# A gated cross-attention and channel-mix kernel: the inverse root of stage two in twelve links on VectorE, right behind the moments, from the second unit on

## The reference

```python
def _layernorm(x, axis=-1, eps=1e-05):
    m = jnp.mean(x, axis=axis, keepdims=True)
    v = jnp.var(x, axis=axis, keepdims=True)
    return (x - m) / jnp.sqrt(v + eps)
...
def _reference_tuple_inner(x, W_r, W_k, W_v, mu_r, mu_k):
    x_prev = jnp.concatenate([jnp.zeros((B, 1, C), x.dtype), x[:, :-1, :]], axis=1)
    xr = mu_r * x + (1.0 - mu_r) * x_prev
    xk = mu_k * x + (1.0 - mu_k) * x_prev
    r = jax.nn.sigmoid(jnp.einsum('btc,dc->btd', xr, W_r))
    k = jnp.einsum('btc,dc->btd', xk, W_k)
    k_act = jnp.square(jax.nn.relu(k))
    out = r * jnp.einsum('btc,dc->btd', k_act, W_v)
...
x = x + jnp.tanh(g_xattn[0]) * _L0_xattn_ref(_layernorm(x, axis=-1), ctx_1024, ctx_1024, mask_SxS2_bk1, ...)
x = x + jnp.tanh(g_ffn[0]) * _L0_ffn_ref(_layernorm(x, axis=-1), L0_ffn_W_r, L0_ffn_W_k, L0_ffn_W_v, L0_ffn_mu_r, L0_ffn_mu_k)
```

## Time and profile before

| what | value |
|---|---|
| median of 3 runs | 1153.17 us (1152.59 to 1156.04) |
| profiled execution, whole | 1153.75 us |
| its span, first to last instruction | 1151.9 us |
| mean granted clock of PE | 0.997 |
| PE busy | 1118.8 us, 97% of the span |
| DVE busy | 888.4 us, 77% |
| ACT busy | 686.3 us, 60% |
| POOL busy | 367.6 us, 32% |

### The profile page before, as it was taken

One profiled execution on the slowest core, in us unless ns is written; L12 is line 12 of the kernel. 1 busy time (PEld: TensorE's weight loads), 2 busy tenths in 40 slices (PEclk: granted clock), 3 DMA queues, 4 the chain that ended last, 5 costly groups with the idle time before them and its releaser, 6 DMA issues.

```text
span 1151.9 us, 21580 instructions
## 1 busy us (share of the span) xinstructions
PE 1118.8 (97%) x7216; PEld 895.2 (78%) x7216; DVE 888.4 (77%) x1964; ACT 686.3 (60%) x1527; POOL 367.6 (32%) x595
## 2 busy tenths in 40 slices
PE   5999999999999999999999999979999999999998
PEld 4677777777778778777877777757888888888886
DVE  7878877888788878887888788867677776776764
ACT  4767776777677767776777677753333323332232
POOL 0153153045045026116214302663442334323331
PEclk9999999999999999999999999989999999999999
DMA  8675575764775676567567557702311132111300
GB/s 284 199 199 146 166 212 153 193 193 132 199 203 131 192 207 171 139 196 214 149 168 211 141 144 229 222 12 74 99 55 56 55 95 71 55 55 62 103 20 37
DMA packets 95709, 162.48 MB, mean 141 GB/s; under 512 B 13296, under 2 KB 22640, under 8 KB 95472
## 3 DMA queue, kind: packets, MB, share of 16 engines
q1 hardware_dynamic: 84912, 143.37, 44.0%
q10 hardware_dynamic: 10688, 17.73, 5.4%
HBM read 109.91 MB, written 49.57 MB: 138 GB/s over the span
## 4 chain that ended last, share of the span: by engine, by line
PE 87%; DMA 3%; issue 2%; DVE 2%; POOL 1%; ACT 1%; SPq 0%; DVEq 0%; ACTq 0%; POOLq 0%
PE bank L550 26%; PE bank L624 18%; PE bank L586 14%; PE bank L615 10%; PE bank L636 9%; PE bank L594 8%; PE bank L749 1%; DMA w_raw<-wvvT 1%; ACT kact_hi L985 1%; PE bank L738 1%; DMA rden_dram<-ctx_sb 0%; DVE xh L1238 0%; POOL w2r_lo L1429 0%; DVE kact L1276 0%; DMA qk_dram<-q_hi 0%
## 5 line engine op out<-in xcount | busy, mean ns | idle before, releaser
L904 ACT ACTIVATE probs<-neg_s,negmax 128x512 f32<-128x512 f32 x512 | 368.1, 720 | 65.0 <-DVE negmax L1079 62.7
L1079 DVE CUSTOM_DVE_ANT_0 neg_s<-bank,mask_big 128x512 f32<-128x512 f32 x512 | 344.0, 679 | 9.7 <-DVE mask_big L1139 1.0
L624 PE MATMUL bank<-ident,probs 128*128 128x128 f32 x2048 | 307.6, 273 | 3.0 <-DVE pT L1085 2.9
L624 PEld LDWEIGHTS bank<-ident,probs 128*128 128x128 f32 x2048 | 248.1, 140 | 51.1 <-issue 6.1
L1085 DVE COPY pT<-bank 128x512 f32<-128x512 f32 x254 | 175.0, 689 | 110.2 <-PE bank L624 109.1
L615 PE MATMUL bank<-k_stack,q_stack 96*128 96x512 f32 x512 | 242.1, 473 | 0.2 <-DMA q_stack<-qk_dram 0.2
L911 ACT COPY pT<-bank 128x512 f32<-128x512 f32 x258 | 149.8, 580 | 127.6 <-PE bank L624 127.0
L636 PE MATMUL bank<-pT,v_sb 128*32 128x512 f32 x1024 | 116.5, 595 | 0.6
L983 ACT ACTIVATE relu<-bank 128x512 f32<-128x512 f32 x32 | 19.2, 599 | 145.3 <-PE bank L550 143.3
L615 PEld LDWEIGHTS bank<-k_stack,q_stack 96*128 96x128 f32 x512 | 97.3, 190 | 1.6 <-DMA q_stack<-qk_dram 0.5
L904 ACT ACTIVATION_READ_ACCUMULATOR probs<-neg_s,negmax 128x1 f32 x512 | 97.1, 190 | 0.0
(11 more groups left out here) (158 smaller groups left out, 2165.3 us busy)
## 6 DMA issues: line engine op xcount, KB each, us to landing
k_stack<-qk_dram SPq DMA_DIRECT2D x93, 256.0 KB, 5.4
q_stack<-qk_dram SPq DMA_DIRECT2D x93, 256.0 KB, 6.2
cT_raw<-ctxT SPq DMA_DIRECT2D x8, 1024.0 KB, 7.6
rden_bc<-rden_dram SPq DMA_DIRECT2D x128, 64.0 KB, 6.2
ctx_dram<-ctx_sb SPq DMA_DIRECT2D x32, 256.0 KB, 2.2
c_raw<-ctx_dram SPq DMA_DIRECT2D x16, 512.0 KB, 5.0
x_in<-x SPq DMA_DIRECT2D x16, 512.0 KB, 5.8
qk_dram<-k_hi SPq DMA_DIRECT2D x31, 256.0 KB, 2.7
```

The source lines that it names most:

```text
L624: mm = nc.tensor.transpose(pt_bank[i % 2][:, a * P:(a + 1) * P], probs[:, i % P_RING, a * P:(a + 1) * P], ident[:])
L904: nc.scalar.activation(probs[:, i % P_RING, :], neg_s[:, i % SM_RING, :], ACT.Exp, bias=negmax[:, k:k + 1], scale=-1.0, accum_out=den[:, g ...
L1079: nc.vector.tensor_tensor_reduce(neg_s[:, i % SM_RING, :], s_bank[tile_no(b, c, i) % S_BANKS][:], mask_big[:, q, :], 1.0, 3e38, ALU.add, A ...
```

## The change

The chain of POOL gets called once only, for the first unit. For all later units `residual_stats` runs a chain on DVE right behind the moments. It is the function that made the very first root, now with its operands as arguments, in twelve links instead of fifteen (the scalar form of an instruction folds the factor -0.5 and the addend 1.5 in). A new semaphore, `root_units`, counts its links. `normalise2` waits for POOL's chain in the first unit alone.

```diff
-            def inverse_root_first():
+            def inverse_root(base, sem_, var, ve, y, t):
...
                 def link(ins):
                     n[0] += 1
-                    ins.then_inc(root_first, 1)
-                    dve.wait_ge(root_first, n[0])
-
-                ve, y, t = var_eps[:], rstd[:], newton[:]
-                link(nc.vector.tensor_scalar(ve, mv[:, :, 1], EPS, None, ALU.add))
+                    ins.then_inc(sem_, 1)
+                    dve.wait_ge(sem_, base + n[0])
+
+                link(nc.vector.tensor_scalar(ve, var, EPS, None, ALU.add))
...
                 for m in range(UM):
                     dve.wait_ge(bn2_done, u * UM + m + 1)
                     nc.vector.bn_aggr(mv2[:, m, :], stats2[:, m, :]).then_inc(mv2_done, 1)
+                if u:
+                    dve.wait_ge(mv2_done, (u + 1) * UM)
+                    inverse_root((u - 1) * CHAIN_FIRST, root_units, mv2[:, :, 1], var_eps2[:], rstd2[:], newton2[:])
...
             def normalise2(b, h):
                 u = b * 2 + h
-                dve.wait_ge(root_chain2, (u + 1) * CHAIN)
+                if u == 0:
+                    dve.wait_ge(root_chain2, CHAIN)
...
-            def inverse_root2(b, h):
-                u = b * 2 + h
-                pool.wait_ge(mv2_done, (u + 1) * UM)
-                inverse_root(u * CHAIN, root_chain2, mv2[:, :, 1], var_eps2[:], rstd2[:], newton2[:])
+            def inverse_root2():
+                pool.wait_ge(mv2_done, UM)
+                inverse_root(0, root_chain2, mv2[:, :, 1], var_eps2[:], rstd2[:], newton2[:])
 
             def step2(b, h):
                 u = b * 2 + h
                 if h and is_last(b):
                     return
-                inverse_root2(*((b, 1) if h == 0 else (b + 1, 0)))
                 if not is_last(b):
                     add_bias(b + 1, h)
```

More of the change, by code:

```diff
@@ L254, in build @@
         rows1_ld, rings_set, root_first = sem("rows1_ld"), sem("rings_set"), sem("root_first")
+        root_units = sem("root_units")
         second_mm, second_hi, second_lo = ([sem(f"{n}_second_{what}") for n in "qk"] for what in ("mm", "hi", "lo"))
@@ L1123, in _ @@
             dve.wait_ge(rings_set, 1)
-            inverse_root_first()
+            inverse_root(0, root_first, mv[:, :, 1], var_eps[:], rstd[:], newton[:])
             for t in range(TT):
@@ L1453, in _ @@
             split_w2(2)
-            inverse_root2(0, 0)
+            inverse_root2()
             first_context(1)
```

## The result

The changed kernel took 1158.45 us in the median of nine runs (1157.67 to 1160.4), against 1154.86 us for nine runs of the kernel before (1152.59 to 1156.04). The ratio is 1.0034, with a 95% interval from 1.0024 to 1.0044. By the ratio that is 3.9 us more (2.8 to 5.1); the two medians differ by 3.6. The forecast was 4.5 us more, inside a range that holds the measured time, and slower by more than 0.3% was its likeliest outcome. All ratios here are of fast executions; two slow ones, of 1399.9 us (kernel before) and 2895.19 us (e12), are left out.

A forecast was written before the change was run, and what follows sets the result against it. TensorE's products bound the kernel, with a short wait for xh each step. Twelve steps at 0.18 (2.2), plus 1.76 for the first and 0.55 for the last, make 4.5 us more: 1157.6, range 1152.5 to 1161.

The forecast's parts named there:

- What bounds a step: Stage two: TensorE's products, plus 0.37 us a step waiting for xh because GpSimd's bias add holds back VectorE's kact_lo.
- The chain's price: Twelve links on VectorE between the moments and mix_r_lo: 2.38 us, 0.198 each, bounds 1.95 and 3.4.
- the rival of free waits: Links on VectorE run at their busy time, chain 1.95 us: 1.5 us less, 1151.7, not slower; chance 0.16.
- The ordinary step: Stage two, from one start of the transposes (T) to the next: 23.74 us against 23.56, 0.18 us more.
- Giving back: In an ordinary step r_proj comes 0.5 us late, which hides T's wait for xh and gives back 0.37 us.
- The late step: The one step of 24.13 us, where x_in lands late (7.7 us at most): no change expected.
- First and last chain: First and last steps of stage two, with no wait for xh to cover the chain: 1.76 and 0.55 us more.
- a small loss: Chain on VectorE between 2.1 and 2.3 us, or a free restart of products: 1 to 3.4 us more; chance 0.17.
- a chain of 1.8 us or less: Chain on VectorE hardly holds r_proj, steps are products alone (23.19 us): about 1149.9, faster by about 0.3%; chance 0.05.
- GpSimd takes the port first: Bias add starts before VectorE's mix_r_lo: 1.9 us more per such step, 1170 if half of thirteen; chance 0.05.

The follow-up runs named there:

- e12: The changed kernel measured again, nothing altered: ratio 1.0028 to the kernel before.
- e2: Kernel before, with GpSimd's bias add of the later batches cut to two columns of a row instead of 512: ratio 0.9944 to the kernel before.
- e5: Changed kernel with nine links in a chain instead of twelve (one Newton round fewer in later units): ratio 0.9969 to the kernel before.
- e6: Changed kernel with fifteen links in a chain instead of twelve (one Newton round more in later units): ratio 1.0121 to the kernel before.
- e7: Kernel before plus a spare twelve-link chain on VectorE ahead of mix_r_lo, writing unread tiles, GpSimd keeping its own chain: ratio 1.0058 to the kernel before.
- e10: As e7, but the spare chain's three tiles placed behind all others of stage one, so no tile moves: ratio 1.0043 to the kernel before.
- e1: Changed kernel with the chain on VectorE behind mix_r_lo instead of ahead of it: ratio 0.9970 to the kernel before.
- e4: Changed kernel with the first of its fifteen chains left on GpSimd: ratio 1.0021 to the kernel before.
- e9: Kernel before with three small tiles reserved but not used, so later tiles lie 8 bytes each further on: ratio 1.0003 to the kernel before.
- e11: As e1, but SP's queue loads x_in ahead of c_raw instead of behind it: ratio 1.0080 to the kernel before.

## Why the prediction was right

- **What bounds a step.** Right. The wait for xh was the bias add's hold on kact_lo: e2 takes it away and gains 6.5 us (4.9 to 8.1), 5.9 by its trace. That is 0.6 more than the 5.3 expected, and most of it is that the floor of a step is 23.15 us and not 23.19.
- **The chain's price.** Right to the hundredth: 2.38 us on two columns, as on four in the earlier trace rows. The links' own durations are 0.16 to 0.17 us on both, and the gaps between them do cost: the rival of free waits falls. e5 and e6 show that each link counts with 0.19 us a step until r_proj is no longer held.
- **The ordinary step.** 23.72 us against 23.74. Its terms were 14.32 (14.31 measured), 0.04 (0.03), 2.38 (2.38), 1.19 (mix_r_lo takes 1.23), 0.20 (0.10) and 5.61 (5.67, which holds the restart). The last three misses, +0.04, -0.10 and +0.06, cancel, and that is luck.
- **Giving back.** Right: r_proj is 0.49 us later, the wait of T is gone, and 0.16 us a step is left. e7 and e10 show the two paths as a maximum and not a sum. They also show what gave back: not the lifted lock but the hold, for with the lock in place a step takes 23.75 us, 0.03 more than without it. In the changed kernel, too, kact_lo is still long in seven steps, and six of them cost nothing.
- **The late step.** Expected without change, it took 23.99 us instead of 24.13. Its x_in is the one that lands last: the add starts 7.66 to 7.84 us after the issue at this same step in the profiles of before, changed, e1 and e12. Those of e4, e5 and e9 have no such step; why not is open.
- **First and last chain.** 1.71 and 0.50 us against 1.76 and 0.55. e4 undoes the first alone.
- **The rivals on a shorter chain.** By time alone a small loss (1 to 3.4 us) isn't excluded: the interval starts at 2.8 us, and the repeat e12 gave 3.2. It is the chain's 2.38 us in the trace that excludes it. What the forecast said of a chain of 1.8 us or less, a gain of 0.3%, came true when e5 made the chain that short: 0.31%.
- **GpSimd takes the port first.** It didn't happen in the changed kernel: the add would have had to start ahead of mix_r_lo, and the closest came 0.94 us behind mix_r_lo's start, so mix_r_lo took 1.23 us in every step. e11 shows the price of such a start, on the chain instead, where the add begins 1.2 us earlier.

## What to carry to other kernels

A chain of tiny dependent instructions costs its start-to-start time (0.198 us a link here), and what matters is which instruction stands behind it: ahead of the one that TensorE waits for, this one cost 0.34%; one instruction later, in VectorE's own wait, the same chain gave 0.3% (e1). Moving the chain off GpSimd was worth something only through the start of the bias add, which then was over earlier in all steps but one, and only where r_proj wasn't held (e1, e5). So ask where GpSimd's remaining large instruction will now start, and what on VectorE stands there: kact_lo, mix_r_lo and the link of e11 all read two tiles in SBUF. Keep that start away from the chain: the order of two loads, which moved it by 1.2 us, turned a gain of 3.5 us into a loss of 9 (e11).

## What the runs showed of the hardware that was not expected

- After TensorE had been held for 2.07 us, its granted clock was 0.70 and 0.54 in the next two stretches (1.7 and 2.6 us), down to the 1.2 GHz level, and 1.00 again after them; after 1.49, 1.51 and 1.52 us at the same place (changed kernel, e7, e10) it stayed at 1.00. It cost 1.55 us in the one profile of e6.
- A link on two columns was stretched from 0.16 to 2.28 us by a GpSimd instruction that had been issued 0.20 us ahead of it, while the link issued at the same moment as GpSimd's took its usual 0.16 (e11).
